# Squared norms of the keys from the diagonal of the gram products, in a gated delta-rule layer

## The reference, cut to what matters

```python
def l2norm(x, eps=1e-06):
    return x * jax.lax.rsqrt(jnp.sum(x * x, -1, keepdims=True) + eps)
...
q = l2norm(q); k = l2norm(k)
q = q * K ** (-0.5)
v_beta = v * beta[..., None]
k_beta = k * beta[..., None]
...
A = jnp.where(strict, -(k_beta @ jnp.swapaxes(k, -1, -2)) * decay, 0.0)
attn = solve_triangular(eyeC - A, eye, lower=True, unit_diagonal=True)
...
out = core * rsqrt(mean(core * core, -1) + EPS) * norm_w
out = out * silu(z)
return out @ w_out
```

## Time and profile before

| | us |
|---|---|
| runs | 1686.71, 1696.61, 1690.67 |
| median of the runs | 1690.67 |
| profiled execution, its time | 1689.3 |
| its span, first to last instruction | 1687.3 |
| TensorE busy | 1475.2 (87%) |
| VectorE busy | 1134.2 (67%) |
| ScalarE busy | 781.5 (46%) |
| GpSimd busy | 391.1 (23%) |
| mean granted TensorE clock | 0.956 of full |

### The profile page before, as it was taken

How to read it: one execution, slowest core, us unless ns; L and a number is a source line. 1 busy time by engine, 2 the same in 40 slices (tenths; PEclk the granted TensorE clock), 3 DMA queues, 4 the chain that set the end, 5 groups by cost and what they waited for, 6 DMA issues and landing times. The chain is left out here.

```text
span 1687.3 us, 22931 instructions
## 1 busy us (share of the span) xinstructions
PE 1475.2 (87%) x8504; PEld 833.0 (49%) x8504; DVE 1134.2 (67%) x2048; ACT 781.5 (46%) x1608; POOL 391.1 (23%) x337
## 2 busy tenths in 40 slices
PE   0025789999999999999999999989699999798998
PEld 0022446657547547547547557566444444344333
DVE  6996675787786786786886886862578777613112
ACT  3133464675676676676676666754121111111111
POOL 7201010402401411311312212214133333100222
PEclk9977887999999999999999999979799999998999
DMA  2001100100100000000000000000301111100011
GB/s 62 0 0 53 38 14 1 38 1 15 38 1 19 33 12 15 26 14 14 25 14 14 26 14 13 1 15 1 102 31 46 46 43 38 67 0 27 27 39 38
DMA packets 15644, 43.02 MB, mean 25 GB/s; under 512 B 3618, under 2 KB 6842, under 8 KB 14394
## 3 DMA queue, kind: packets, MB, share of 16 engines
q1 hardware_dynamic: 15546, 41.69, 7.2%
HBM read 39.58 MB, written 2.10 MB: 25 GB/s over the span
## 5 line engine op out<-in xcount | busy, mean ns | idle before, releaser
L973 DVE SCALAR_TENSOR_TENSOR conv<-bank,taps,conv 128x510 f32<-128x510 f32 (+2 forms) x384 | 283.5, 744 | 74.6 <-ACT conv L755 65.1
L448 PE MATMUL bank<-rT,wf 128*128 128x512 f32 x512 | 264.1, 633 | 41.0 <-DMA wf<-in_wf_dram 33.2
L1409 ACT ACTIVATE ffn_relu<-bank 128x512 f32<-128x512 f32 x100 | 59.7, 597 | 300.6 <-PE bank L1548 300.6
L1548 PE MATMUL bank<-rT,ffn_chunk 128*128 128x512 f32 x400 | 193.1, 607 | 0.0
L1567 PE MATMUL bank<-ffn_weighted,ffn_chunk 128*128 128x512 f32 x400 | 190.7, 600 | 1.8 <-DVE ffn_weighted L1526 1.8
L1380 POOL TENSOR_TENSOR ffn_relu<-ffn_relu 128x512 f32<-128x512 f32 x96 | 108.3, 1128 | 245.4 <-ACT ffn_relu L1409 245.4
L1526 DVE TENSOR_TENSOR ffn_weighted<-ffn_relu,bank 128x512 f32<-128x512 f32 x96 | 65.9, 688 | 145.9 <-POOL ffn_relu L1380 133.8
L448 PEld LDWEIGHTS bank<-rT,wf 128*128 128x128 f32 x512 | 92.5, 197 | 128.2 <-issue 108.4
L1130 POOL TENSOR_TENSOR sq<-sq,qsq 128x512 f32<-128x512 f32 x64 | 81.4, 1272 | 285.6 <-ACT sq L918 283.8
L1548 PEld LDWEIGHTS bank<-rT,ffn_chunk 128*128 128x128 f32 x400 | 77.8, 195 | 97.5 <-issue 97.4
L755 ACT ACTIVATE conv<-bank,taps 128x512 f32<-128x512 f32 x128 | 88.4, 711 | 81.0 <-PE bank L448 80.6
(11 more groups left out here) (254 smaller groups left out, 2787.4 us busy)
## 6 DMA issues: line engine op xcount, KB each, us to landing
ffn_chunk<-in_L_chunks_dram SPq DMA_DIRECT2D x25, 512.0 KB
wf<-in_wf_dram SPq DMA_DIRECT2D x8, 1024.0 KB, 4.8
wz<-in_wz_dram SPq DMA_DIRECT2D x8, 512.0 KB, 3.3
wo<-in_wo_dram SPq DMA_DIRECT2D x8, 512.0 KB, 3.3
ffn_spread<-in_L_spread_dram SPq DMA_DIRECT2D x33, 40.0 KB
side<-in_fT_dram SPq DMA_DIRECT2D x1, 1024.0 KB, 5.1
xT<-in_xT_dram SPq DMA_DIRECT2D x1, 1024.0 KB, 8.8
gate_dram<-gate SPq DMA_DIRECT2D x1, 1024.0 KB, 3.9
```

What stands on the lines that cost most here:

```text
L448: ins = pe.matmul(banks[b][:], wf[:, c, n // NH, :], rT[:, c, halves(n % NH)], start=(c == 0), stop=(c == CT - 1))
L973: dve.scalar_tensor_tensor(acc[:, :, k:], src[:, :, 0:T - k], taps[:, n // NH, KS - 1 - k:KS - k], acc[:, :, k:], ALU.mult, ALU.add).then_inc(
L1548: last = pe.matmul(banks[h][:], chunk[:, slot, c, t * P:(t + 1) * P], rT[:, c, halves(h)], start=(c == 0), stop=(c == CT - 1))
```

## The change

The squares, the one-column products and their waits go away. VectorE reads the squared norms from the diagonal of the gram products, in the gram stage, once for each `n`: two `scalar_tensor_tensor` instructions multiply 128x128 of a bank by the identity and sum along the row into `ksum` (the accumulator output), then three small instructions form `ccol` for that `n` only: add eps, reciprocal, multiply by `beta`. Each waits for the one ahead of it. ScalarE's `root_k` is now once a group (128x16), right after `take_blocks`, and makes only `inv_u`. The logarithm no longer gives 1/norm^2. `rms(g, 0)` and `rms(g, 1)` wait for convolutions of the next group instead of `lk_done`, which guards the banks 6 and 7 that they write.

```diff
-        def k_norm(p, kh):
-
-            pe.wait_ge(ksq_ready, p * 4 + 2 * kh + 2)
-            for tt in range(TT):
-                last = pe.matmul(banks[6 + kh][:, tt:tt + 1], ksq[:, tt // 4, tt % 4 * P:(tt % 4 + 1) * P],
-                                 ones[:, 0:1], start=True, stop=True)
-            last.then_inc(knorm_full, 1)
...
             gram(g, 0)
             pe.wait_ge(sel_ready, g + 1)
-            if first:
-                pe.wait_ge(lk_done, 2)
-            else:
+            if not first:
                 pe.wait_ge(ln_done, before)
             decay(g, 0)
...
                     elif not last_group:
-                        pe.wait_ge(lk_done, p * GK + n - 1)
+                        pe.wait_ge(conv_ready, p * NF * NH + 5 + n)
...
                 if not last_group and n >= 1:
                     project_v(p, n - 1)
-                    if n < 3:
-                        pe.wait_ge(conv_ready, p * NF * NH + 6 + n)
-                        k_norm(p, n - 1)
...
-        for kh in range(GK):
-            pe.wait_ge(conv_ready, 7 + kh)
-            k_norm(0, kh)
         groups(pe, group)
...
-        def square_k(p, kh):
-            act.wait_ge(feat_ready, p * NF * NH + 4 * kh + 4)
-            for h in range(NH):
-                act.activation(ksq[:, h, :], feat[:, 2 * kh + 1, halves(h)], ACT.Square).then_inc(ksq_ready, 1)
-
-        def root_k(p, kh):
-
-            act.wait_ge(knorm_full, p * GK + kh + 1)
-            act.activation(lk[:, kh, :], banks[6 + kh][:, 0:TT], ACT.Ln, bias=EPS).then_inc(lk_done, 1)
-            act.wait_ge(lk_done, p * GK + kh + 1)
-            act.activation(u2[:, kh, :], lk[:, kh, :], ACT.Exp, scale=-1.0)
-            act.activation(iu[:, kh, :], lk[:, kh, :], ACT.Exp, scale=0.5).then_inc(u_ready, 1)
+        def root_k(g):
+
+            act.activation(lk[:], ksum[:], ACT.Ln, bias=EPS).then_inc(lk_done, 1)
+            act.wait_ge(lk_done, g + 1)
+            act.activation(iu[:], lk[:], ACT.Exp, scale=0.5).then_inc(u_ready, 1)
...
             take_blocks(g, 1, range(2, 4), 16)
+            root_k(g)
...
-        def scale_heads(p):
-            dve.wait_ge(u_ready, (p + 1) * GK)
-            dve.wait_ge(heads_done, p * 2 + 1)
-            dve.tensor_tensor(ccol[:].rearrange("p (k r) t -> p k r t", k=GK),
-                              bcol[:].rearrange("p (k r) t -> p k r t", k=GK),
-                              u2[:].unsqueeze(2).to_broadcast([P, GK, 2, TT]), ALU.mult).then_inc(heads_done, 1)
+        def scale_heads(g, n):
+
+            kh, s = n // B, n % B
+            b0, b1 = (2, 3) if n % 2 == 0 else (0, 1)
+            for of, t in ((banks[b0][:, T:T + P], 2 * s), (banks[b1][:, P:2 * P], 2 * s + 1)):
+                last = dve.scalar_tensor_tensor(norms[:, t % 2, :], of, 1.0, ident[:], ALU.mult, ALU.mult,
+                                                accum_out=ksum[:, kh, t:t + 1])
+            last.then_inc(scaled, 1)
+            dve.wait_ge(scaled, g * 3 * GK * B + 3 * n + 1)
+            dve.tensor_scalar(u2[:, kh, 2 * s:2 * s + 2], ksum[:, kh, 2 * s:2 * s + 2], 1e-6, None,
+                              ALU.add).then_inc(scaled, 1)
+            dve.wait_ge(scaled, g * 3 * GK * B + 3 * n + 2)
+            dve.reciprocal(u2[:, kh, 2 * s:2 * s + 2], u2[:, kh, 2 * s:2 * s + 2]).then_inc(scaled, 1)
+            dve.wait_ge(scaled, g * 3 * GK * B + 3 * n + 3)
+            dve.tensor_tensor(ccol[:, 2 * kh:2 * kh + 2, 2 * s:2 * s + 2], bcol[:, 2 * kh:2 * kh + 2, 2 * s:2 * s + 2],
+                              u2[:, kh:kh + 1, 2 * s:2 * s + 2].to_broadcast([P, 2, 2]), ALU.mult).then_inc(heads_done, 1)
+            dve.wait_ge(heads_done, g * (GK * B + 1) + n + 2)
...
                 dve.wait_ge(gram_full, g * GK * B + n + 1)
+                scale_heads(g, n)
                 for r in range(2):
```

More of the change, by code:

```diff
@@ L370, in delta_phase @@
     qsq = sb("qsq", [P, GK, NT])
-    lk, u2, iu = (sb(n, [P, GK, TT]) for n in ("ln_k2", "u2", "inv_u"))
+    ksum, lk, u2, iu = (sb(n, [P, GK, TT]) for n in ("k2", "ln_k2", "u2", "inv_u"))
+    norms = sb("norms", [P, 2, P])
     z = sb("z", [P, GV, TT, HD])
@@ L394, in delta_phase @@
     wf_in, wz_in, wo_in, small_in = (sem(n) for n in ("wf_in", "wz_in", "wo_in", "small_in"))
-    proj_full, turn_full, gram_full, decay_full, gate_full, stage_full, cross_full, mix_full, rms_full, knorm_full, \
+    proj_full, turn_full, gram_full, decay_full, gate_full, stage_full, cross_full, mix_full, rms_full, \
         out_full = (sem(n + "_full") for n in (
-            "proj", "turn", "gram", "decay", "gate", "stage", "cross", "mix", "rms", "knorm", "out"))
-    conv0_ready, feat_ready, qsq_ready, ksq_ready, lk_done, u_ready, dec_ready, zs_ready, z_ready, evicted, sq_ready, \
+            "proj", "turn", "gram", "decay", "gate", "stage", "cross", "mix", "rms", "out"))
+    conv0_ready, feat_ready, qsq_ready, scaled, lk_done, u_ready, dec_ready, zs_ready, z_ready, evicted, sq_ready, \
         ln_done, rs_ready = (sem(n) for n in (
-            "conv0_ready", "feat_ready", "qsq_ready", "ksq_ready", "lk_done", "u_ready", "dec_ready", "zs_ready",
+            "conv0_ready", "feat_ready", "qsq_ready", "scaled", "lk_done", "u_ready", "dec_ready", "zs_ready",
             "z_ready", "evicted", "sq_ready", "ln_done", "rs_ready"))
@@ L852, in group @@
                 act.activation(zs[:, n // NH, halves(n % NH)], banks[n % 4][:], ACT.Silu).then_inc(zs_ready, 1)
-            act.wait_ge(u_ready, (g + 1) * GK)
+            act.wait_ge(u_ready, g + 1)
             for n in range(NU):
@@ L926, in group @@
                     act.preload_act_table_set("natural_log_exp_and_others")
-                if not last_group:
-                    if n == 0:
-                        square_k(p, 0)
-                    if n == 1:
-                        root_k(p, 0)
-                        square_k(p, 1)
-                    if n == 2:
-                        root_k(p, 1)
             root(g, first, NU - 2)
@@ L949, in scalar @@
         act.preload_act_table_set("natural_log_exp_and_others")
-        for kh in range(GK):
-            square_k(0, kh)
-            root_k(0, kh)
         groups(act, group)
@@ L1007, in group @@
                 take_taps(p)
-            dve.wait_ge(heads_done, g * 2 + 2)
+            dve.wait_ge(heads_done, g * (GK * B + 1) + 1)
             if not first:
@@ L1106, in group @@
                 fill(HF + n)
-            if not last_group:
-                scale_heads(p)
         dve.wait_ge(small_in, 32)
@@ L1114, in vector @@
         take_heads(0)
-        scale_heads(0)
         groups(dve, group)
```

1 line of the change is left out of this document (removed).

## The result

The changed kernel takes 1764.11 us in the median (1757.71 to 1770.66), the kernel before 1688.69 us beside it. The ratio is 1.0453, with a 95% interval of 1.0371 to 1.0535: slower by 4.5%, where 1745 us was forecast. The four times of the changed kernel stand on two levels, two at 1758 and two at 1770 us. The profiled execution is one of the lower level: 1757.71 us, span 1755.9, mean granted clock 0.92 where it was 0.956.

The account below looks back on a forecast made before the run. TensorE and VectorE were both taken as close to the limit in the gram stage, with VectorE's chain bounding the inversion. 1689.3 + 13.8 + 41.1 = 1744.2 us profiled, 1745 for the median; range 1698 to 1782.

Parts of the forecast that it names:

- Removed: Mix stage, groups 0 to 6: one-column products gone, -23.9 us; ahead of group 0: first `m` at about 185.4, gain 10.4 us.
- The rival of savings that land elsewhere: Mix stage held by another engine's chain, so the 3.42 us return only in part; half gone, +12 us; no chance given.
- The chain: VectorE, gram stage: two diagonal products and three small instructions added for each `n`, taken as 1.35 us.
- the forecast 13.8 us for the work: Whole kernel without the clock: -23.9 - 10.4 + 42.0 + 6.1 = +13.8 us, giving 1703.1.
- the rival "faster": Gram stage: added VectorE instructions mostly overlapped; at 0.9 us for each `n`, clock safe and 1675 us; chance 0.05.
- Gram stage: VectorE sets the pace without waiting: step 3.45 us, groups 1 to 7 27.6 instead of 21.6 us, +42.0 in sum.
- The wait: TensorE at line 534, before the transposed inverse: idle time grows from 0.99 by 1.3 to 2.3 us.
- How many lose it: Behind line 534: three of groups 1 to 6 lose the clock, 13.7 us each, +41.1; 2 to 4 lost had chance 0.40.
- two rivals: Groups 1 to 6 behind line 534: none or one loses the clock, 1703 to 1717 us, 0.27; or five or six, 0.17.
- The rival of nearly every group: Groups 1 to 6 behind line 534: five or six lose the clock, since groups repeat closely; 1772 to 1785 us; chance 0.17.
- Loses it again: Group 0 behind line 534: had lost the clock before the change and loses it again, so nothing is added.
- the clock's part: Behind line 534: three of groups 1 to 6 at 13.7 us each, +41.1 us; groups 0 and 7 add nothing.

## Why the prediction was right, and where it was not

*Removed.* The first `m` of group 0 starts at 185.38 us; 185.4 was forecast. In the mix stage `mix` follows on `project_v` directly, and the run without the chain gained 22.0 us in the groups 0 to 6, where the removed work was priced at 23.9. The rival of savings that land elsewhere, with half of them gone, falls.

*The chain.* Forecast 1.35 us, measured 1.14. The terms: diagonal products 0.21 and 0.33 (to the next start) instead of 0.27 and 0.38, reciprocal 0.20 instead of 0.24, product with `beta` 0.20 instead of 0.21, the accumulator nothing instead of 0.05. The Trainium skill's rule ("VectorE: DVE Perf Modes", "Two Vector instructions with no wait between them") that an accumulator output makes two instructions is confirmed by the rows of `DVE_READ_ACCUMULATOR`, 0.08 us each; the 0.16 us for a chain that I had worked out from it are not on the path. Of the forecast 13.8 us for the work, the chain's error takes off 64 x 0.21 = 13.4, and the slow instruction adds 7 x 0.75 = 5.3, which makes 5.7; 9.1 was found. Of the 3.4 us between them 1.9 are the removed work (22.0 for 23.9), and about half of that goes with the waits in front of `below32`, which in the run without the chain were 1.07 to 1.09 us instead of 0.90 to 0.99. The other 1.5 us I have not placed. The chain is a hundredth longer than the 1.13 us at which the sum without the clock would be nothing, so on the work alone the rival "faster" came closer than I had thought; against it stood an instruction of 0.92 us that I had not foreseen.

*Gram stage.* No idle time in front of `m`, as forecast. The step is 3.25 instead of 3.45 us, the stage 26.7 instead of 27.6.

*The wait.* 2.3 us was forecast, 2.12 to 2.15 measured in the groups 1 to 6. This is the step on which all hangs, and it was right for partly other reasons. The load of the last gram product of group 1 in the changed kernel, as in the earlier trace rows:

```profile
328.16 0.30 PEld L487 LDWEIGHTS bank<-feat 128*128 128x128 f32 x2 [1.04 <-DVE m L1002]
```

From it to the end of the last `m` it is now 334.51 - 328.16 = 6.35 us, up by 0.6 from 5.8, where 6.9 was forecast. But TensorE's own part, from the load to the start of the wait, became shorter by more than the 0.24 us that I had counted: from (382.22 - 0.99) - 346.48 = 34.75 us to (364.57 - 2.13) - 328.16 = 34.28, so by 0.47. From the end of the last `m` to the first product of `below32` it is 0.1 us longer (364.57 - 334.51 = 30.06 instead of 382.22 - 352.26 = 29.96). The three make the 1.14 us by which group 1's wait grew; forecast were 1.3.

*The clock at 0.50.* The prediction called 30.7 us at 0.50 beside a busy engine an agreement with the rule that activity releases the clock. Taken alone these rows do not show it, since the engine was reported as busy all the time. What agrees is the run with eight large products behind the wait, which had the clock back after 3.4 us.

*How many lose it.* Three were forecast, six did. Taking half of the groups was a guess between two rivals, and it failed. The rival of nearly every group was right in its count, and its argument was the better one: the waits of the groups repeat within hundredths, 2.12 to 2.15 us. That it was still not certain is shown by the waits of 1.86 and 2.08 us that went either way. The price of 13.7 us was read from line 534 to the first norm product; over a whole period it is 12.1 to 13.0.

*Group 0.* "Loses it again" was wrong. It waits for 2.04 us instead of 2.43 and keeps the clock: 13 us that I had not counted. The chain is not what shortens this wait, since without any chain it is 2.06 us; what does is not shown. With 6 x 12.1 for 3 x 13.7 the clock's part is 59.5 instead of 41.1 us. The errors have opposite signs: 72.5 for 41.1 in the groups 1 to 6 is 31.4 too little, 13.0 for group 0 and 13.8 - 9.1 = 4.7 for the work are too much. Together 1744.2 + 31.4 - 13.0 - 4.7 = 1757.9, and the profiled execution took 1757.7. So the wait and what it does to the clock were right; that the forecast of 1745 lies only 19 us below the median, with half of the losses counted, was luck in part.

*Group 7.* Its wait is 6.4 us, and 5.2 in the kernel before; no feature products stand behind it, and the clock is lost near it in both (20.5 and 17.1 us at 0.50). From its first `m` to the end the change costs 5.5 us, where the chain and the slow instruction make 5.1 (6.0 - 8 x 0.21 + 0.75). Leaving it out of the clock's part was right.

Two things stay open. What decides between two waits of the same length was not found. It is not the program alone: up to the wait of group 0 the changed kernel and the run with eight products behind the wait are the same program, and 2.04 us kept the clock in the one execution while 1.97 lost it in the other. And the two levels of the changed kernel, 12 us apart, fit one loss more or less, but only executions of the lower level were profiled, and the mean granted clock does not settle it: it is 0.92 twice on the lower level and 0.914 and 0.922 on the upper one. The kernel before has such times too, 1676.93 and 1675.93 us among times that mostly lie between 1687 and 1693, which fit a group 0 that kept its clock and were not profiled either.

## What to carry to other kernels

Before work is moved to an engine whose chain another engine waits for, look at what the waiting engine does afterwards: here 1.2 us more of idle time on TensorE cost twelve, because small products stood behind it. Price the wait by the granted clock behind such waits in the trace, and if it is in doubt, put a little useful or useless work in front of the wait; and give the kernel before the same help when the two are compared. Done so (chain one instruction shorter, its first one moved, two products ahead of the wait), the change pays: 1667.7 us against 1675.5 for the kernel before with its own two products, and 1689 for it as it was. That is 7.8 us or half a per cent in its favour; the change as it was first made, without that help, costs 4.5%.

## What the runs showed of the chip

- **A wait of about 2 us loses the clock, but not by its length alone.** In the groups 0 to 6 of the profiled executions, all waits at this place up to 1.6 us kept it and all from 2.10 us on lost it. Between 1.74 and 2.08 us they went both ways: kept eleven times (from 1.74, over 1.86 and 2.04, to 2.08), lost nine times (from 1.76, over 1.85 and 1.97, to 2.08). The lower bound is weaker than the upper one, since six of ten executions with a single product ahead of group 0's wait, none of them profiled, stand where a loss after about 1.6 us would put them.
- **What runs behind decides on the price.** The small products, with feature products between them, left the clock at 0.50 for 27 to 31 us; eight large ones ahead of them had it back after 3.4. The loss costs about 12 us in the one case and 1.7 in the other.
- **Small VectorE instructions can be held by GpSimd.** A `TENSOR_SCALAR` and `TENSOR_TENSOR`s of two to four elements a partition took 0.71 to 0.92 us instead of 0.17, and ended with GpSimd's product, in each of the groups 1 to 7. A reciprocal, and `m` and the diagonal products with one input in PSUM, were not held. Nor was the product with `beta` in the changed kernel, 0.16 us at 309.50 beside a GpSimd `memset` from 309.42 to 310.37, which reads nothing. The Trainium skill states it in "SBUF — State Buffer", section "Who interferes with whom": a `tensor_scalar` in a two-port mode, or a `tensor_tensor` with both inputs in SBUF beside a GpSimd instruction that reads SBUF, contends with GpSimd for a shared port pair, and the one that comes second waits until the first is done. The trace agrees, at 0.75 us a group, though no run shows in which mode the `tensor_scalar` ran; I had not looked for it in the stage where the chain was to go.
- **The accumulator of a VectorE instruction cost nothing on the path here.** Its read took 0.08 us, beside the next diagonal product or, behind the second one, up to 308.31 us, where that product itself ended at 308.30.
